# Product keys on Trainium2: the eight gathered rows of a token are weighted and summed on TensorE by diagonal matrices, instead of on VectorE

## The reference

```
q = (x @ w_q).reshape(b, n, 2, 8, 64).transpose(2, 0, 1, 3, 4)      # x is layer-normalised
sim = einsum('pbnhd,hkpd->pbnhk', q, keys)                          # 32 similarities per head and half
# the best of sx + sy over all pairs: index = 32 * argmax(first half) + argmax(second half)
h = einsum('bnd,bnhkd->bnhk', x, w_down[indices])                   # one row per head: 8 dot products a token
h = gelu(h) * relu(scores)
return einsum('bnhk,bnhkd->bnd', h, w_up[indices])                  # 8 rows of 128 weighted and summed
```

## Time and profile before

| | us |
|---|---|
| median of 3 runs | 1663.72 (1660.70 to 1664.81) |
| the profiled execution | 1674.48 |
| its span, first to last instruction | 1672.0 |
| PE busy | 1123.6 (67%) |
| DVE busy | 1042.1 (62%) |
| POOL busy | 587.0 (35%) |
| ScalarE busy | 524.1 (31%) |
| mean granted clock of PE | 0.784 |

### The profile page before, as it was taken

The page is one execution under the profiler, slowest core; times in us unless marked ns, Lnnn a source line. Parts: engine busy times, 40 slices in busy tenths (PEclk is TensorE's granted clock), DMA queues, the critical chain, the costliest instruction groups (busy, mean ns, idle before and its releaser), DMA issues. The chain is left out here.

```text
span 1672.0 us, 26006 instructions
## 1 busy us (share of the span) xinstructions
PE 1123.6 (67%) x9324; PEld 733.6 (44%) x9324; DVE 1042.1 (62%) x2995; ACT 524.1 (31%) x1045; POOL 587.0 (35%) x680
## 2 busy tenths in 40 slices
PE   1467988787868964556463399788648987856510
PEld 0333434343347963556463288433337943322200
DVE  2455676767643435999999466455434445668896
ACT  0123434443424532222221133144314513423300
POOL 7033323223341551101032544201345521256674
PEclk9978889998879985555555599888958997867665
DMA  4920000000032224444260112230002210022232
GB/s 118 314 69 1 1 1 1 1 1 13 11 101 70 71 77 113 101 113 113 64 153 14 42 58 61 67 110 1 17 27 63 72 59 13 11 79 81 83 102 73
DMA packets 74245, 106.19 MB, mean 64 GB/s; under 512 B 11501, under 2 KB 55712, under 8 KB 71616
## 3 DMA queue, kind: packets, MB, share of 16 engines
q1 hardware_dynamic: 59968, 72.16, 16.0%
q0 software_dynamic: 14144, 32.32, 6.4%
HBM read 77.10 MB, written 27.33 MB: 62 GB/s over the span
## 5 line engine op out<-in xcount | busy, mean ns | idle before, releaser
L856 POOL DMA_INDIRECT y_d<-arena,goal x138 | 132.6, 961 | 174.1 <-DVE arena L939 100.6
L1694 DVE CUSTOM_DVE_ANT_0 arena<-ps,far 128x512 f32<-128x512 f32 (+3 forms) x256 | 116.6, 488 | 64.3 <-PE ps L1379 62.6
L2033 POOL DMA_INDIRECT wide<-in_w_ud,arena x128 | 130.1, 1016 | 75.2 <-DVE arena L2064 38.8
L2953 PE MATMUL ps<-wide,arena 78*128 78x32 bf16 x3840 | 110.6, 187 | 47.7 <-ACT wide L3066 34.1
L2953 PEld LDWEIGHTS ps<-wide,arena 78*128 78x128 bf16 x3840 | 109.4, 104 | 54.3 <-ACT wide L3066 38.0
L1015 PEld LDWEIGHTS ps<-arena 128*128 128x128 f32 (+1 forms) x1012 | 123.3, 191 | 4.1
L1015 PE MATMUL ps<-arena 128*128 128x128 f32 (+1 forms) x1012 | 123.6, 274 | 0.0
L1296 POOL TENSOR_SCALAR_AFFINE_SELECT arena<-arena 128x520 f32<-128x520 f32 (+1 forms) x64 | 41.1, 654 | 154.9 <-ACT arena L1567 154.8
L1567 ACT ACTIVATE arena<-ps 128x1024 f32<-128x1024 f32 x80 | 78.4, 1022 | 50.9 <-PE ps L1400 50.6
L1379 PE MATMUL ps<-fr 32*128 32x256 f32 (+3 forms) x256 | 84.1, 409 | 14.1 <-DVE arena L1694 11.0
L1006 PE MATMUL ps<-arena 128*128 128x256 f32 x368 | 89.7, 387 | 1.6 <-DVE arena L915 1.6
(11 more groups left out here) (514 smaller groups left out, 2570.2 us busy)
## 6 DMA issues: line engine op xcount, KB each, us to landing
arena<-low_d SPq DMA_DIRECT2D x32, 780.0 KB
xs_d<-zrow SPq DMA_DIRECT2D x1, 10320.0 KB, 39.8
arena<-xs_d SPq DMA_DIRECT2D x69, 129.0 KB, 2.1
arena<-y_d SPq DMA_DIRECT2D x16, 256.0 KB, 3.3
arena<-in_w SPq DMA_DIRECT2D x2, 1408.0 KB
y_d<-arena,goal POOLq DMA_INDIRECT x138
wide<-in_Wfc SPq DMA_DIRECT2D x1, 2048.0 KB, 11.9
wide<-in_Wproj SPq DMA_DIRECT2D x8, 256.0 KB, 6.7
```

Source lines behind the costliest of these rows:

```text
L856: pool.indirect_dma_start(out=y_d, in_=yb[:, i % 2, c, :], in_offset=None, out_offset=bass.IndirectOffsetOnAxis(ap=goal[:, i % 4, c:c + 1] ...
L1694: ins = nc.vector.tensor_tensor_reduce(junk[:, n % 2, 384 * i:384 * i + w], ps[:, n % 2, 384 * i:384 * i + w], far[:, T - w:T], 1.0, 3 * N ...
L2033: pool.indirect_dma_start(out=rows_g[t % 4][:, h, :], out_offset=None, in_=A["w_ud"], in_offset=bass.IndirectOffsetOnAxis(ap=eidi[:, t % 8 ...
L2953: mm = nc.tensor.matmul(ps[:, 2 * (i % 3) + h // 2, col:col + 4 * HD], ring[m_ % 4][:, h * NK + p_, t % 2 * P:t % 2 * P + P], table[n // 4 ...
```

## The change

The weighted sum moves to PE. `weigh` (DVE) computes only the eight weights. `diagonals` (ScalarE) writes eight matrices of 128x128 float32: the identity, scaled in each partition by that token's weight for head h. `up` (PE) multiplies each with the up half of the gathered rows and sums all eight in one PSUM bank. `add` (DVE) is one addition of that bank to x. The diagonals have two sets of places, in memory whose earlier contents are no longer needed, so diagonals(t) waits for up(t - 2). The gathered rows get a fifth buffer, and gather(t) now waits for the addition of tile t - 5. `up` is a new use of the two PSUM banks in turn.

The core of the diff:

```diff
-                if t >= 4:
-                    pool.wait_ge(k["added"], t - 3)
+                if t >= 5:
+                    pool.wait_ge(free7_dve, added(t - 5))
                 for h in range(PKH):
-                    pool.indirect_dma_start(out=rows_g[t % 4][:, h, :], out_offset=None, in_=A["w_ud"],
+                    pool.indirect_dma_start(out=rows_g[t % 5][:, h, :], out_offset=None, in_=A["w_ud"],
...
-            def add(dve, ch, t):
+            def weigh(dve, t):
                 dve.wait_ge(k["act"], acted(t))
-                ch.link(nc.vector.tensor_tensor(hv[:, t % 4, :], act_h[:, t % 4, :], esc[:, t % 8, :], ALU.mult))
+                nc.vector.tensor_tensor(hv[:, t % 4, :], act_h[:, t % 4, :], esc[:, t % 8, :], ALU.mult).then_inc(k["hv"], 1)
+
+            def add(dve, arrived, t):
+                src = arrived("up", t)
+                nc.vector.tensor_tensor(xa[:, t, :], xa[:, t, :], src[:, 0:D], ALU.add).then_inc(free7_dve, 1)
+
+            def added(t):
+                return emptied(place["up", t])[1]
+
+            def diagonals(act, t):
+                act.wait_ge(k["hv"], t + 1)
+                if t >= 2:
+                    act.wait_ge(turn7, place["up", t - 2] + 1)
                 for h in range(PKH):
-                    ins = nc.vector.scalar_tensor_tensor(xa[:, t, :], rows_g[t % 4][:, h, D:2 * D], hv[:, t % 4, h:h + 1], xa[:, t, :],
-                                                         ALU.mult, ALU.add)
-                    if h < PKH - 1:
-                        ch.link(ins)
-                ins.then_inc(k["added"], 1)
+                    ins = nc.scalar.activation(diag[t % 2][h // 4][:, h % 4, :], ident[:, :], ACT.Identity, scale=hv[:, t % 4, h:h + 1])
+                ins.then_inc(k["diag"], 1)
+
+            def up(pe, take, t):
+                k_ = take("up", t)
+                pe.wait_ge(rows_in[t % 4], 16 * PKH * (t // 4 + 1))
+                pe.wait_ge(k["diag"], t + 1)
+                for h in range(PKH):
+                    mm = nc.tensor.matmul(ps[:, k_, 0:D], diag[t % 2][h // 4][:, h % 4, :], rows_g[t % 5][:, h, D:2 * D],
+                                          start=h == 0, stop=h == PKH - 1)
+                mm.then_inc(turn7, 1)
...
@@ tensor, in a round, behind maximum_rows(G + 1)
+                    if keys_after and G >= 10:
+                        K_.up(pe, take, G - 10)
...
@@ tensor, behind the rounds
                     for t in range(LOOPED + 2, NTT):
                         K_.similar(pe, take, t)
+                        K_.up(pe, take, t - 6)
+                    for t in range(NTT - 6, NTT):
+                        K_.up(pe, take, t)
...
@@ scalar, at the end of a round, behind similar_out and gelu
+                    if keys_after and G >= 10:
+                        K_.diagonals(act, G - 10)
...
@@ scalar, behind the rounds
                     K_.similar_out(act, arrived, LOOPED + 1)
+                    K_.diagonals(act, 6)
                     K_.gelu(act, 8, 9)
                     K_.turned(act, arrived, B - 1)
+                    K_.diagonals(act, 7)
                     for t in range(9, NTT):
                         if t + 3 < NTT:
                             K_.similar_out(act, arrived, t + 3)
                         K_.gelu(act, t, t + 1)
+                        K_.diagonals(act, t - 1)
+                    K_.diagonals(act, NTT - 1)
...
@@ vector, at the end of a round
                         K_.choose(dve, ch, G - 6)
+                    if keys_after and G >= 10:
+                        K_.add(dve, arrived, G - 10)
                     if keys_after and G >= 9:
-                        K_.add(dve, ch, G - 9)
+                        K_.weigh(dve, G - 9)
...
@@ vector, behind the rounds
                     K_.dot(dve, ch, 8)
-                    K_.add(dve, ch, 7)
+                    K_.weigh(dve, 7)
                     K_.normed(dve, B - 1)
                     for t in range(LOOPED + 1, NTT):
                         K_.choose(dve, ch, t)
+                        K_.weigh(dve, t - 3)
+                        if t >= LOOPED + 2:
+                            K_.add(dve, arrived, t - 6)
                         K_.dot(dve, ch, t - 2)
-                        K_.add(dve, ch, t - 3)
                     for t in range(NTT - 2, NTT):
                         K_.dot(dve, ch, t)
-                        K_.add(dve, ch, t - 1)
-                    K_.add(dve, ch, NTT - 1)
+                        K_.weigh(dve, t - 1)
+                        K_.add(dve, arrived, t - 4)
+                    K_.weigh(dve, NTT - 1)
+                    for t in range(NTT - 4, NTT):
+                        K_.add(dve, arrived, t)
```

More of the change, by code:

```diff
@@ L49 @@
 Blocks = namedtuple("Blocks", "sync last_rows gpsimd results settled vector combine tensor scalar")
-Keys = namedtuple("Keys", "rstd gather stats normed choose dot add store turn similar turned similar_out gelu")
+Keys = namedtuple("Keys", "rstd gather stats normed choose dot add store turn similar turned similar_out gelu weigh diagonals up")
 Parts = namedtuple("Parts", "sync gpsimd vector tensor scalar ahead_gpsimd ahead_vector ahead_tensor ahead_scalar")
@@ L618, in build @@
                                           "hot", "pv", "out", "shift", "w", "vw", "o")}
-        k = {n: sem("k_" + n) for n in ("stats", "mean", "rstd", "xn", "turn", "xnT", "sim", "seen", "idx", "dot", "act", "hv", "added")}
+        k = {n: sem("k_" + n) for n in ("stats", "mean", "rstd", "xn", "diag", "seen", "idx", "dot", "act", "hv", "added")}
         i0 = {n: lsem("i0_" + n) for n in ("qm", "s", "a", "c", "m", "p", "t", "pt", "o", "turn", "y")}
@@ L2008, in product_keys @@
         def product_keys(place, emptied, finished):
+            old_rows = arena[:, 14400 + 4 * 2 * D:14400 + 4 * 2 * D + PKH * 2 * D]
             at[0] = 14400 + 4 * 2 * D + B * NT * RW + T
+            diag = [wq_rows[:, :, :, :].rearrange("p a b c -> p (a b c)")[:, 0:PKH * P].rearrange("p (h c) -> p h c", h=PKH)]
+            diag = [[diag[0][:, 0:4, :], diag[0][:, 4:8, :]], [ws1[:, :].rearrange("p (h c) -> p h c", h=4), ws2[:, :, :]]]
             sims = carve(2, 2 * PKH * PKN); best = carve(16, PKN); ranked = carve(16, PKN); prod = carve(PKH, D)
@@ L2016, in product_keys @@
             rows_g = [wide_rows[j // 2][:, j % 2 * PKH * 2 * D:(j % 2 + 1) * PKH * 2 * D].rearrange("p (h d) -> p h d", h=PKH) for j in range(4)]
+            rows_g.append(old_rows.rearrange("p (h d) -> p h d", h=PKH))
             PAIRED = 8
@@ L2084, in store @@
+            def up(pe, take, t):
[6 more added lines that the diff above has]
+                mm.then_inc(turn7, 1)
             def store(sp):
                 for t in range(NTT):
-                    sp.wait_ge(k["added"], t + 1)
+                    sp.wait_ge(free7_dve, added(t))
@@ L2116, in product_keys @@
             return Keys(rstd=rstd, gather=gather, stats=stats, normed=normed, choose=choose, dot=dot, add=add, store=store, turn=turn,
-                        similar=similar, turned=turned, similar_out=similar_out, gelu=gelu)
+                        similar=similar, turned=turned, similar_out=similar_out, gelu=gelu, weigh=weigh, diagonals=diagonals, up=up)
         def cross_attention(i, blocks):
@@ L2169, in cross_attention @@
                     plan("mz", G + 1)
+                if keys_after and G >= 10:
+                    plan("up", G - 10)
             if keys_after:
@@ L2181, in cross_attention @@
                 for t in range(LOOPED + 2, NTT):
-                    plan("ps", t)
+                    plan("ps", t); plan("up", t - 6)
+                for t in range(NTT - 6, NTT):
+                    plan("up", t)
             if routes:
                 plan("pl", 2); plan("rt", 3); plan("lg", 3); plan("pl", 3)
-            by_dve = ("mz", "o", "y", "lg", "pl")
+            by_dve = ("mz", "o", "y", "lg", "pl", "up")
             place = {key: n for n, (key, _) in enumerate(uses)}
```

2 lines of the change are left out of this document (1 added, 1 removed).

## The result

The changed kernel took 1670.57 us (median of 5 runs, 1669.59 to 1673.47), the kernel before beside it 1662.54 (5 runs, 1660.70 to 1664.81): ratio 1.005, 95% interval 1.0035 to 1.0065, so 8.0 us slower. The profiled execution took 1669.59, its span is 1667.9.

What follows compares the result with a forecast made beforehand. No engine as a whole was taken as the bound: gathers set the last 80 us, and DVE first, with PE and ScalarE close, the attention rounds. 1663.7 + 9.4 (tail) - 4 (rounds) = 1669.1, said as 1669; range 1657 to 1679.

Steps and rivals of the forecast that it cites:

- scores more than 13 us apart: Attention rounds: score starts were forecast 9.5 to 12 us apart; more than 13 would show the prediction wrong.
- Gather(11) behind add(6): Start of the tail: gather(11) waits for add(6), which stands behind choose(12) in DVE's queue; costs 1.6 us.
- Gather(15) behind add(10): Tail: the last gather waits for add(10), behind dot(14), leaving POOL 4.9 us idle instead of 0.3; costs 4.7 us.
- Behind the last dot: End of the tail: weights, two tiles' diagonals, two up and an addition take 9.5 us instead of 6.4; costs 3.1.
- The tail: From the statistics of batch 3 to the end: two gather waits and the work after the last dot cost 9.4 us.
- The rounds: Attention rounds before the tail: 12 us won by relieving DVE, less 8 for PE's lower clock, give 4 us.
- the diagonals' price: ScalarE, each tile: eight diagonal activations take 1.6 us, between bounds of 1.4 and 2.8.
- the Exp table: ScalarE in odd rounds, after the Gelu: 0.5 us was put for loading the table of Exp.
- DVE sets everything: Rival, before the tail: DVE alone sets the pace, tiles' choices come 18 us earlier; 1655 us, chance 0.15.
- PE stays fast: Rival, rounds: up fills the pauses in which PE's clock fell, rounds give 8 to 12 us; 1662 us, chance 0.22.
- PE is slow: Rival, rounds: PE's clock is low half the stretch or more, rounds lose 0 to 6 us; 1676 us, chance 0.23.

Runs made afterwards that it cites:

- the edited kernel before: Kernel before the change, with tile 14's eight sums moved ahead of dot(15): 1658.71 us, ratio 0.9972 to the kernel before.
- the changed kernel again: The changed kernel, nothing altered, run once more on chip B: 1665.13 us, ratio 1.0009 to the kernel before.
- the diagonals early: Changed kernel, rounds' diagonals ahead of ScalarE's similarity copy and Gelu: 1682.05 us (chip A), 1681.09 (C); ratios 1.0065, 1.007 to the kernel before.
- all edits: Changed kernel with earlier additions, rounds' diagonals ahead of copy and Gelu, tile 14 finished before dot(15), tile 15 summed on DVE: 1647.95 us; repeat 1647.64.
- e1: Changed kernel, behind the rounds add(t - 6) ahead of choose(t), add(10) and add(11) ahead of dot(14) and dot(15): 1682.77 us, ratio 1.0073 to kernel before.

## Why the prediction came out, point by point

The forecast was 1669 in 1657 to 1679, with slower and no change nearly even; 1670.6 is inside, and slower is right. That it was slower and not the same owes something to luck: the chances were 0.43 to 0.42, the sum of 1669.1 lay 0.4 us beyond the edge between them, and on chip B the same two kernels can't be told apart. By one of its own signs the prediction was wrong: it named scores more than 13 us apart, and those of rounds 11 and 13 stand 13.4 and 15.2 us ahead of the next. That belongs to the term of the rounds below. The terms:

- **Gather(11) behind add(6), +1.6**: the gap is 1.43 us, 1.1 more than between two issues. Right.
- **Gather(15) behind add(10), +4.7**: 5.52 less 0.30 is 5.2. Right in place and size.
- **Behind the last dot, +3.1**: 9.3 us against 6.5, +2.8. Right in sum, by errors that cancel: the diagonals take 2.44, not 1.6, and `up(13)` comes here too, since the alternation of two PSUM banks, which the sum left out, ties it to add(11); but PE reached the higher clock in the meantime (granted 0.50 up to 1661 and 1.00 from 1662; 2.50 and 2.02 instead of 3.4). The 2.0 and 3.8 us that the sums use for an `up` at the higher and the lower clock are an estimate from the earlier trace rows, where sixteen records take 1.95 us at a granted 1.00 and eight take 2.07 at 0.50; the tail has the 3.8 because the earlier trace rows show 0.50 there. The runs showed 2.02 to 2.05 for an `up` at 1.00 and 3.75 to 3.78 at 0.50.
- **The tail, +9.4**: 86.0 against the undisturbed 77.9, +8.1. The two waits are 6.3, but the last dot ends only 5.3 later. **The gathers' own time**, for which I had taken no change, accounts for that: from the start of gather 11 to that of gather 14 it is 32.1 us in the edited kernel before (24 issues, gaps 0.3) and 31.2 in the changed kernel again, 0.3 us a tile, and gathers 14 and 15 are 0.7 and 0.2 shorter. But gather 10 went the other way, 10.85 us against 10.04, so 1.0 us is the sum. The runs don't isolate a cause.
- **The rounds, 4 us won**: 93.6 to 92.4, **1.2 won: this term was mis-sized.** The working had 11.5, 9.5, 13, 10 and 19.5 us from the scores of round 11 on with PE always at the higher clock; 13.4, 12.5, 15.2, 11.9 and 21.0 came, 10.5 more, for which 8 us of lower clock had been set aside. The step that failed is the diagonals' price. Eight take 2.44 us, near the upper bound of 2.8: one lasts 387 ns in the mean, and the next starts 0.30 us after it started; I had taken the pace of two PSUM copies, 0.16, for that of 128x128 activations, though L1578's 0.35 stood beside it. In five rounds that is 4.2 us, more than the 2.8 by which the term missed. A smaller part is the Exp table, for which I had put 0.5 in odd rounds: its 1.28 us came in round 12 (ScalarE 1519.93), where PE's wait for the copy grew from 0.80 to 1.57, and were hidden beside `up` at 1543.08. And what won the 1.2 was tile 6 alone; tiles 0 to 5 lost 3.0. With the diagonals early rounds 11 and 12 take 9.3 and 10.1, near my 9.5 for an even round, but this is another order of ScalarE's queue than the one I priced. The changed kernel has its diagonals in line behind copy and Gelu, and the longest two of the pauses that this leaves on PE, 4.1 us each, stand before an `up` at the lower clock.
- **DVE sets everything** (1655) was wrong as I put it, DVE waiting in the rounds for PE before five of six additions, up to 4.1 us; behind the last scores it did set the pace in the kernel before (add(6) above). **PE stays fast** (1662) and **PE is slow** (1676) did not happen: the granted clock rose from 0.71 to 0.83 in the rounds. With all edits it was 0.89, and the rounds gave 16.5 us.

The traces make 8.1 - 1.2 = 6.9 us, where the sum had 9.4 - 4 = 5.4; 8.0 was measured (5.8 to 10.8 by the interval), and 2.8 on chip B, where the interval also holds no change. That the change made the program slower is well supported by the first measurement and the traces; that it is 8 us on every chip is not.

## What to carry to other kernels

Taking work off a busy engine is not enough: here tiles 0 to 5 took some 17 us of additions off DVE and made the rounds longer, since PE then waited 2.6 to 4.1 us in each of rounds 11 to 14 for the operand that ScalarE makes. Eight small ScalarE instructions moved ahead of a copy and a Gelu were worth 15 us in the rounds, more than the whole change cost, on the two chips without unexplained waits; on the other two, alone, they brought no gain in the total. When a buffer's release moves behind a step that waits for the next transfer (add(10) behind dot(14)), the transfer after that waits too, here 5.52 us. Compare stretches of traces bounded by the same instruction when totals scatter by more than the effect.

## What the runs showed that I had not expected

On chips A and C, all seven kernels have waits of ScalarE and VectorE for products that PE's records show long ended, up to 10.2 us each; labelled "remote" they are 4 to 12 a kernel after 1440 us, 14 to 48 us in sum over both engines; on B and D, and in the changed kernel's first profile, there is none. The kernel before is slower on those chips too (1670.7 and 1668.1 against 1662.4 and 1661.8). The 6.33 us of the earlier trace rows are of this kind. Two of these waits end when the traffic of a tile's gather has ended (1539.82 above right behind it, 1655.42 in e1 some 2.5 us later), but the one that ends at 1534.89 does so in the midst of such traffic (131 GB/s from 1534 to 1536). So a link with the gathers is not shown, and no run took the gathers away: the cause is open. The changed parts stood 0.4 to 0.9% above the kernel before on these chips, against 0.1% for the whole change on chip B. That the handovers between PE and its neighbours, which this change adds twice a tile, cost more there is a guess that no run tests.
